# Nine products of hats on VectorE in a fused residual and deformable convolution block

## What is computed

```python
out = conv(x, w1)
out = jax.nn.relu(group_norm(out, gn1_scale, gn1_bias))
om = conv(out, w_off, pad=1) + b_off[None, :, None, None]
off_x = om[:, :K]
off_y = om[:, K:2 * K]
mask = jax.nn.sigmoid(om[:, 2 * K:])
...
py = grid_y[None] + off_y
px = grid_x[None] + off_x
sampled = bilinear_sample(out, py, px) * mask[:, None]
out = jnp.einsum('bckhw,ock->bohw', sampled, w2.reshape(w2.shape[0], w2.shape[1], K))
out = jax.nn.relu(group_norm(out, gn2_scale, gn2_bias))
out = conv(out, w3)
out = group_norm(out, gn3_scale, gn3_bias)
return jax.nn.relu(out + x)
```

## Time and profile before

| | us |
|---|---|
| median of 3 runs | 2959.81 (2959.12 to 2959.93) |
| the profiled execution | 2959.69 |
| its span, first to last instruction | 2957.9 |
| TensorE busy | 2910.1 (98%) |
| VectorE busy | 2355.7 (80%) |
| ScalarE busy | 1796.4 (61%) |
| GpSimd busy | 252.8 (9%) |

### The profile page before, as it was taken

How to read it: one execution, slowest core, us unless ns; L and a number is a source line. 1 busy time by engine, 2 the same in 40 slices (tenths; PEclk the granted TensorE clock), 3 DMA queues, 4 the chain that set the end, 5 groups by cost and what they waited for, 6 DMA issues and landing times.

```text
span 2957.9 us, 46557 instructions
## 1 busy us (share of the span) xinstructions
PE 2910.1 (98%) x16518; PEld 2869.1 (97%) x16518; DVE 2355.7 (80%) x5000; ACT 1796.4 (61%) x3281; POOL 252.8 (9%) x209
## 2 busy tenths in 40 slices
PE   9999999999998899999999999999999999999997
PEld 9999999999997899999999999999999999999997
DVE  5655889865666688888888888888888888888885
ACT  4544332346665466767667676676766767667664
POOL 0000000000000011111111111111111101111110
PEclk9999999999999899999999999999999999999998
DMA  7774111035653445444444444444445444444431
GB/s 270 216 238 133 44 44 44 10 121 218 248 229 130 123 135 156 152 151 158 150 158 152 149 158 149 159 150 150 158 147 163 147 149 158 149 158 152 150 118 74
DMA packets 209208, 437.39 MB, mean 148 GB/s; under 512 B 18640, under 2 KB 170192, under 8 KB 203344
## 3 DMA queue, kind: packets, MB, share of 16 engines
q1 hardware_dynamic: 159408, 326.82, 32.8%
q10 hardware_dynamic: 49568, 107.60, 11.8%
HBM read 307.71 MB, written 126.64 MB: 147 GB/s over the span
## 4 chain that ended last, share of the span: by engine, by line
PE 65%; DVE 2%; DMA 1%; ACT 1%; SPq 0%; issue 0%; POOL 0%; ACTq 0%; DVEq 0%; POOLq 0%
PE sample L87 7%; PE deform L87 7%; PE sample L88 7%; PE sample L92 7%; PE deform L92 7%; PE deform L88 7%; PE work L87 6%; PE work L92 6%; PE work L88 6%; PE work L74 1%; PE work L76 1%; PE work L75 1%; PE work L2051 1%; DMA hats<-hat_scratch 1%; PE sums_ps L1135 0%; PE work L2040 0%
## 5 line engine op out<-in xcount | busy, mean ns | idle before, releaser
L1465 ACT ACTIVATE v_hi<-sample 128x392 fp32r<-128x392 f32 (+1 forms) x640 | 292.1, 463 | 313.3 <-PE sample L92 304.5
L87 PE MATMUL sample<-s_hi,aT_hi 98*128 98x392 f32 (+1 forms) x1280 | 417.9, 332 | 8.2 <-DVE v_lo L1824 8.1
L88 PE MATMUL sample<-s_hi,aT_lo 98*128 98x392 f32 (+1 forms) x1280 | 414.2, 329 | 0.0
L87 PE MATMUL deform<-v_hi,w_w 128*128 128x392 f32 x1152 | 402.9, 350 | 0.0
L88 PE MATMUL deform<-v_hi,w_w 128*128 128x392 f32 x1152 | 392.6, 341 | 0.0
L1824 DVE TENSOR_TENSOR v_lo<-sample,v_hi 128x392 fp32r<-128x392 f32 (+1 forms) x640 | 327.1, 519 | 64.5 <-ACT v_hi L1465 63.0
L92 PE MATMUL sample<-s_lo,aT_hi 98*128 98x392 f32 (+1 forms) x1280 | 315.4, 327 | 0.0
L92 PE MATMUL deform<-v_lo,w_w 128*128 128x392 f32 x1152 | 310.4, 341 | 0.5 <-DVE v_lo L1824 0.4
L1456 ACT ACTIVATE s_hi<-hats 98x784 fp32r<-98x784 f32 x288 | 245.6, 853 | 100.2 <-DVE x L1712 71.9
L1816 DVE TENSOR_TENSOR s_lo<-hats,s_hi 98x784 fp32r<-98x784 f32 x288 | 278.8, 968 | 2.5 <-ACT s_hi L1456 1.6
L87 PEld LDWEIGHTS sample<-s_hi,aT_hi 98*128 98x128 f32 x1280 | 242.2, 189 | 11.6 <-issue 5.5
(11 more groups left out here) (226 smaller groups left out, 7308.9 us busy)
## 6 DMA issues: line engine op xcount, KB each, us to landing
hats<-hat_scratch SPq DMA_DIRECT2D x768, 150.1 KB
x<-in_x SPq DMA_DIRECT2D x64, 784.0 KB, 6.0
in_home<-y_scratch ACTq DMA_DIRECT2D x248, 196.0 KB, 3.1
out<-x ACTq DMA_DIRECT2D x62, 784.0 KB, 4.4
y_home<-in_x SPq DMA_DIRECT2D x32, 784.0 KB, 5.0
y_scratch<-y_out SPq DMA_DIRECT2D x16, 1568.0 KB, 5.9
terms<-in_x SPq DMA_DIRECT2D x30, 784.0 KB, 4.6
y_scratch<-y_home SPq DMA_DIRECT2D x15, 1568.0 KB, 5.1
```

What stands on the lines that cost most here:

```text
L87: nc.tensor.matmul(out, w_hi, x_hi, start=start, stop=False)
L88: nc.tensor.matmul(out, w_lo, x_hi, start=False, stop=False)
L1465: nc.scalar.activation(v_hi[:, group % 2, c, 0:taps_of(g), i, :], sample[:, t % 2, 0:cols(g)].rearrange("p (k s) -> p k s", s=PIX), ACT.Co ...
```

## The change

`BY_POOL` and GpSimd's `make_s` are taken out, with their two calls in GpSimd's step. VectorE makes products 6 and 7 as well: `make_s(now, 6)` stands behind `rest_s(now, 5)`, `make_s(now, 7)` behind `rest_s(now, 6)`, both in the ordinary step and in the one of the first pair. VectorE's wait for GpSimd's count ahead of product 8 goes, as all products are now made by one queue.

```diff
-BY_POOL = (6, 7)
...
         def _(pool):
             @of_pair
-            def make_s(p, u):
-                unit = UNITS * p.n + u
-                n, slot = 2 * PIX, unit % HATS
-                if u - 1 not in BY_POOL:
-                    pool.wait_ge(s_made, unit)
-                pool.wait_ge(hats_loaded[slot], loads_until(p, u))
-                nc.gpsimd.tensor_tensor(hats[:, slot, 0:2, 0:n], hats[:, slot, 0:2, 0:n],
-                                        hats[:, slot, 2:3, 0:n].broadcast_to([HALF, 2, n]), ALU.mult).then_inc(s_made, 1)
...
                 root(now, gn1)
-                make_s(before, 6)
-                make_s(before, 7)
                 mask_hats(now)
...
             def make_s(p, u):
                 unit = UNITS * p.n + u
                 n, slot = 2 * PIX, unit % HATS
-                if (u - 1) % UNITS in BY_POOL:
-                    dve.wait_ge(s_made, unit)
                 dve.wait_ge(hats_loaded[slot], loads_until(p, u))
...
                 rest_s(now, 5)
+                make_s(now, 6)
                 rest_v(now, 7)
...
                 rest_s(now, 6)
+                make_s(now, 7)
                 rest_v(now, 10)
```

More of the change, by code:

```diff
@@ L1668, in make_s @@
             @of_pair
-            def make_s(p, u):
-                unit = UNITS * p.n + u
-                n, slot = 2 * PIX, unit % HATS
-                if u - 1 not in BY_POOL:
-                    pool.wait_ge(s_made, unit)
-                pool.wait_ge(hats_loaded[slot], loads_until(p, u))
-                nc.gpsimd.tensor_tensor(hats[:, slot, 0:2, 0:n], hats[:, slot, 0:2, 0:n],
-                                        hats[:, slot, 2:3, 0:n].broadcast_to([HALF, 2, n]), ALU.mult).then_inc(s_made, 1)
-            @of_pair
             def mask_hats(p):
```

## The result

The changed kernel takes 3010.06 us (median of 4 runs, 3007.68 to 3011.03), the one before 2959.47 in the same comparison (2958.28 to 2959.93): a ratio of 1.017, 95% interval 1.0156 to 1.0184. It is 1.7% slower. Forecast were 3009 us with a range of 2984 to 3016. The profiled execution took 3011.03 us with a span of 3009.2, against 2959.69 and 2957.9 before.

The account below looks back on a forecast made before the run. TensorE, busy 98% of the span, was taken as the bound. Pairs 1 to 30 growing 0.83 + 0.78 = 1.61 us each (48.3), plus about 0.8 in pair 0, gave 49.1 us on 2959.69: 3008.8 us, range 2984 to 3016.

Parts of the forecast that it names:

- TensorE has nothing to give, and rest_v(11) meets tile 13 on the point: Deformable-stage pairs: TensorE has no idle time; its load for tile 13 starts 0.05 us behind VectorE's rest_v(11).
- Product 6 costs nothing: Behind rest_s(5): VectorE idles 1.33 us for the offset products, more than the 0.89 us product 6 costs.
- Product 7 costs 0.83 us a pair: Behind rest_s(6), no VectorE idle time up to rest_v(11): tile 13 starts 0.83 us later, bounds 0.79 and 0.89.
- rival A: The mask beside gn3 holds nobody: 30 x 0.83 + 0.8 = 25.7, giving 2985.4 us; chance 0.37.
- The mask holds L1122 or L1125 for 0.78 us a pair: VectorE's gn3 steps now start inside GpSimd's mask product and are held 0.78 us a pair, bounds 0 and 1.01.
- Pair 0 costs 0.8 us: First pair: shorter chain, but tile 12 loads right behind rest_v(10); loses about 0.8 us (0 to 0.89), no mask hold.
- rival D: Loads of products 6 and 7 late on VectorE, or further collisions or lowered clock: above 3016 us; chance 0.06.
- Pair 31 costs nothing, and keeps its length: Last pair: no offsets or mask to make, VectorE idles ahead of rest_v(10) and rest_s(7); costs 0 (to 0.1) us.
- The sum: Pairs 1 to 30 each grow 0.83 + 0.78 = 1.61 us; with pair 0, 49.1 us on 2959.69: 3008.8 us.
- a pair now takes 63.1 us, as said: Sign: distance between the same steps of two pairs grows from 61.5 us to 63.1 (rival A: 62.4).
- C: Rival, not slower: VectorE's idle time absorbs product 7 as it does product 6, 2959.7 us; chance 0.04.

Follow-up runs that it names:

- small mask: The changed kernel with GpSimd's mask product cut to 4 of 196 pixels an image, so most of the mask is left out: 2987.12 us, ratio 1.0092.
- late mask: The changed kernel with one more wait on GpSimd, so the mask product starts only after the reduce of gn3: 2984.55 us, ratio 1.0084.
- product 7 alone: The kernel before with only product 7 moved to VectorE, product 6 staying on GpSimd: 3010.67 us, ratio 1.0172.

## Why the prediction was right

- *TensorE has nothing to give, and rest_v(11) meets tile 13 on the point*: right. The 0.05 us between them (0.04 to 0.06) holds in all 30 pairs of both kernels, and what was put ahead of rest_v(11) or taken away since came out in the time, in both directions.
- *Product 6 costs nothing*: right, shown by itself (0.9997), and its 0.89 us seen to leave a 1.33 us wait.
- *Product 7 costs 0.83 us a pair*: right, at the low end of its bounds (0.79 to 0.89). With the small mask the kernel is 2987.12 us, with the late mask 2984.55; rival A's sum for this was 2985.4. From the first load of pair 1 to that of pair 31 both kernels take 0.79 us a pair more than the one before. The step from L1776 to tile 12 grew by 0.44 us (1948.72 - 1942.93 = 5.79, before 5.35), where 0.38 was worked out.
- *The mask holds L1122 or L1125 for 0.78 us a pair* (0.64 to 1.01): right, 0.80, or 0.77 a pair by the time between the changed kernel and the two with product 7 alone to pay for (1.56 - 0.79). What the trace of before couldn't show, that GpSimd holds VectorE as VectorE holds GpSimd, is shown now: a held step of 0.20 us ends 0.05 us behind the mask, which fits its being let go some 0.15 us before the mask's recorded end, where 0.13 was assumed. That L1122 and the mask would start within 0.03 us of each other was worked out; which of them comes first was not, and the 0.78 lay between the two cases (0.89 and 0.72 measured), of which the runs gave 15 pairs each. That the two cases came out even is luck.
- *Pair 0 costs 0.8 us*: right for the gap, too small for the pair. From the first sample load of pair 0 to that of pair 1 (964.29 and 1023.88 after, 963.47 and 1021.01 before) it is 59.59 - 57.54 = 2.05 us. The gap ahead of tile 12 grew from 1.16 us to 2.03, that is by 0.87:

```profile
1001.47 0.19 PEld L86 LDWEIGHTS sample<-s_hi,aT_hi 98*128 98x128 f32 x1 [2.03 <-issue]
1001.00:1006.00 5.00, 4.50 (x17) 4.53 (x18) 3.20 (x5) 3.68 (x7) 1.02 (x1) 0.69 0.28 78
```

  Behind it TensorE ran at the lower clock for a while: in the stretch from 1001 to 1006 us (second line, in the form of the earlier trace rows) the granted clock is 0.69, before it was 1.00. Tile 12 is 0.48 us later than before when counted from the first load of the pair, tile 13 is 2.04, so this stretch costs 1.56 us. (Ahead of the gap the changed kernel had gained some 0.4 us, as the clock rose at other times in the two kernels.) All seven kernels here with product 7 at this place have a gap of 2.03 or 2.04 us in pair 0, and the clock fell behind it in three of them (the changed one, product 7 alone, late mask). I had set a lowered clock aside with rival D.
- *Pair 31 costs nothing, and keeps its length*: right for product 7, wrong for the pair. From tile 11 to tile 14, the stretch of product 7, it takes 10.36 us after (2951.32 to 2961.68) and 10.37 before (2899.85 to 2910.22). But from its first load to tile 14 it takes 44.50 us (2917.18 to 2961.68) where it took 42.64 (2867.58 to 2910.22), 1.86 more. 1.54 of that lies between tiles 5 and 6, in a stretch at the lower clock, far ahead of the moved product:

```profile
2928.00:2931.00 3.00, 3.00 (x11) 3.00 (x10) 1.21 (x6) 0.91 (x2) 0.00 (x0) 0.50 0.64 215
```

  The kernel before has the upper clock there. This pair is full of short gaps, and it has a stretch at the lower clock in the kernel before too (0.56 from 2887 to 2890 us); in the kernel with the late mask it has none in the same steps. No run ties this part to the change, and its cause stays open.
- *The sum.* Pairs 1 to 30 took 46.7 us more (first load of pair 1 to that of pair 31: 2917.18 - 1023.88 = 1893.30, before 2867.58 - 1021.01 = 1846.57), 1.56 a pair where 1.61 was forecast; a pair now takes 63.1 us, as said. Some 1.2 us of the difference is in one pair, 23, in which the kernel before waited 1.25 us for v_lo. With pair 0's 2.05, pair 31's 1.86 and 0.82 us of difference ahead of the stage, less 0.16 at the end, that is the 51.3 us between the two spans. So the mechanism of the 30 pairs carries the forecast, and that the total came within 2 us of 3009 is in part luck: 1.6 us too much for the 30 pairs, and 3 us of lowered clock in pairs 0 and 31 that were in no term.
- *The rivals.* A was half of the truth and fell with the second half: 2985 us is what the kernel takes when the mask is out of the way, and one wait gets it there. C fell with the time itself: every kernel with product 7 at this place takes 2984 us or more. Of D the late load fell: VectorE's idle time ahead of its products that waits for loads is 10.6 us in all, less than the 14.7 before. The lowered clock that D also held came, but weighs 3 us and not the 7 that would have left the range.

One rule of the Trainium skill that I weighed (SBUF — State Buffer, "Who interferes with whom") has been tested by this: a VectorE step with two SBUF inputs is held by a GpSimd step that reads SBUF and started first, and one with a single SBUF input is not. Beside the mask the first held one of the two steps in all 30 pairs of the changed kernel, and the second held in 29 pairs of the kernel before. That L1712 passed inside a root, in 29 pairs of the kernel before, does not fit the rule: a root reads 2 elements a partition. That the hold ends with the reading and not with the instruction would explain it; no run here separates the two for a root.

## What to carry to other kernels

An engine that is 80% busy may still be the one that sets the time at one point of the loop: look for the wait whose release and release-taker lie 0.05 us apart in every iteration, and price a moved step by the idle time between its new place and that point, not by the engine's total. Collect all the idle time on that path, also that behind other engines' waits, before saying what is left over. And when a step moves VectorE against GpSimd in time, list which two-input steps of VectorE newly fall inside a GpSimd instruction: it was half of the loss here, and ordering the two engines by one wait took it back.

## What the runs showed of the hardware

- A VectorE step of 0.20 us lasted 0.92 to 1.09 us because GpSimd's product of 1.04 us had started first, 1.58 to 1.74 us beside one of 1.69 to 1.76 us, 0.50 to 0.67 us beside one of 0.61 to 0.69 us. The profile books the hold as busy time of the held step; no wait row names it.
- Hundredths of a us in the start order decide who is held. With the mask 0.03 to 0.04 us ahead (product 7 alone) L1122 was held in all 30 pairs. With recorded starts within 0.01 us of each other, L1121 slipped through in 15 of the 30 pairs of the changed kernel and GpSimd's instruction was then longer (1.11 instead of 1.04 us), and L1124 was held instead.
- TensorE's granted clock fell to its lower level for some ten matrix products (0.33 instead of 0.18 us each) behind gaps of 1.71 to 1.87 us in 19 of 30 pairs, behind gaps of 1.83 to 1.90 in 7 of 14, behind gaps of 2.03 or 2.04 in pair 0 in 3 of 7 kernels, and in none of 30 pairs behind gaps of 1.04 to 1.22 us. Where it fell, it cost about 1.5 us on top of the gap.
